# Attention and mixture of experts on one core: routing and expert slots in one block, half of the kept row added into each slot output

## The reference

```python
x = _layernorm(x + attention(x, ...))                 # x: (4, 512, 512)
top_vals, top_idx = jax.lax.top_k(x_flat @ w_router, 2)
probs = softmax(top_vals)                             # two gates per token
h = square(relu(einsum('nc,ecd->ned', x_flat, w_fc)))
y = einsum('ned,edc->nec', h, w_proj)
x = _layernorm(x + sum over the two experts of probs * y)
```

## Time and profile before

| what | value |
|---|---|
| median of 3 runs | 1528.96 us (1528.15 to 1529.29) |
| profiled execution, its own time | 1526.92 us |
| span of the profile | 1525.3 us |
| PE, PEld busy | 94%, 79% |
| DVE, ACT, POOL busy | 50%, 48%, 28% |
| mean granted clock of PE | 0.974 |
| accumulating gathers, issue to landing | 5.4 / 5.9 / 6.2 us |
| output stores of 256 KB, median issue to landing | 2.2 us |
| 2 MB weight loads, raw and rounded, median issue to landing | 9.4 and 8.3 us |

### The profile page before, as it was taken

How to read it: one execution, slowest core, us unless ns; L and a number is a source line. 1 busy time by engine, 2 the same in 40 slices (tenths; PEclk the granted TensorE clock), 3 DMA queues, 4 the chain that set the end, 5 groups by cost and what they waited for, 6 DMA issues and landing times. The chain is left out here.

```text
span 1525.3 us, 26299 instructions
## 1 busy us (share of the span) xinstructions
PE 1429.1 (94%) x7936; PEld 1210.1 (79%) x7937; DVE 770.0 (50%) x1784; ACT 728.3 (48%) x1633; POOL 421.5 (28%) x417
## 2 busy tenths in 40 slices
PE   7999999999999999999999998799999579999980
PEld 5888888888888888888888887588888468888870
DVE  6555555655555655655655554345545433333323
ACT  5655565655655655655655655222222123333333
POOL 1221212211222121221221211143233333543376
PEclk9999999999999999999999999899999789999995
DMA  4112112021111121111111120735445267556499
GB/s 154 50 40 62 36 53 62 28 62 48 41 62 48 41 62 48 41 48 62 41 48 62 41 70 21 274 143 206 170 173 190 93 214 248 193 190 237 150 180 207
DMA packets 71979, 160.23 MB, mean 105 GB/s; under 512 B 14096, under 2 KB 14736, under 8 KB 69520
## 3 DMA queue, kind: packets, MB, share of 16 engines
q1 hardware_dynamic: 61168, 109.55, 22.0%
q0 software_dynamic: 10784, 50.36, 11.0%
HBM read 107.36 MB, written 52.52 MB: 105 GB/s over the span
## 5 line engine op out<-in xcount | busy, mean ns | idle before, releaser
L317 POOL TENSOR_TENSOR small<-small,half 128x4 f32<-128x4 f32 x193 | 194.6, 1008 | 761.8 <-DVE small L346 761.8
L434 DVE CUSTOM_DVE_ANT_0 logit<-score_ps,bias 128x128 f32<-128x128 f32 (+3 forms) x256 | 124.8, 487 | 156.8 <-PE score_ps L531 118.8
L269 ACT ACTIVATE prob<-logit,small 128x128 f32<-128x128 f32 (+3 forms) x256 | 144.2, 563 | 118.5 <-DVE small L434 114.7
L544 PEld LDWEIGHTS y_ps<-vs,prob_t 128*128 128x128 f32 x1280 | 174.9, 191 | 21.9 <-ACT prob_t L276 4.5
L544 PE MATMUL y_ps<-vs,prob_t 128*128 (+1 forms) x1280 | 185.2, 276 | 1.0 <-ACT prob_t L276 0.7
L276 ACT ACTIVATE prob_t<-prob_ps 128x128 f32<-128x128 f32 (+3 forms) x256 | 111.5, 436 | 53.3 <-PE prob_ps L537 52.3
L766 ACT ACTIVATE yt_hi<-turn_ps,subln 128x512 fp32r<-128x512 f32 x64 | 44.0, 688 | 168.8 <-PE turn_ps L1031 156.2
L537 PE MATMUL prob_ps<-ident,prob 128*128 128x128 f32 x640 | 112.8, 274 | 3.3 <-ACT prob L269 3.2
L488 PE MATMUL k_ps<-w_hi,x_hi 128*128 (+1 forms) x256 | 103.9, 406 | 5.9 <-DVE w_lo L385 5.8
L1040 PE MATMUL out_ps<-w_hi,yt_hi 128*128 128x512 f32 x256 | 107.5, 420 | 1.9 <-DVE yt_lo L872 1.9
L488 PE MATMUL v_ps<-w_hi,x_hi 128*128 (+1 forms) x256 | 107.0, 418 | 0.0
(11 more groups left out here) (174 smaller groups left out, 3268.3 us busy)
## 6 DMA issues: line engine op xcount, KB each, us to landing
y_scratch<-x_now SPq DMA_DIRECT2D x65, 256.0 KB, 2.9
x_raw<-in_x_t SPq DMA_DIRECT2D x64, 256.0 KB, 2.8
y_raw<-y_scratch SPq DMA_DIRECT2D x15, 1024.0 KB
w_raw<-in_w_experts POOLq DMA_DIRECT2D x7, 2048.0 KB, 9.4
w_hi<-in_w_experts POOLq DMA_DIRECT2D x7, 2048.0 KB, 8.3
w_raw<-in_w_all SPq DMA_DIRECT2D x16, 768.0 KB, 5.6
slots_y<-zeros SPq DMA_DIRECT2D x13, 768.0 KB
xs<-slots_x SPq DMA_DIRECT2D x39, 256.0 KB
```

The source lines that it names most:

```text
L269: nc.scalar.activation(prob[:, 0:width], logit[:, 0:width], ACT.Exp, scale=-1.0, bias=least[:, h:h + 1], accum_out=row_sum[:, (i % 2) * HG ...
L317: nc.gpsimd.tensor_tensor(r, ms, half[:, :], ALU.pow).then_inc(ready, 1)
L434: nc.vector.tensor_tensor_reduce(out=logit[:, 0:width], in0=score_ps[:, 0:width], in1=bias[:, h, T - width:T], scale=1.0, scalar=3e38, op0 ...
L544: mm = nc.tensor.matmul(y_ps[:, h * D:(h + 1) * D], prob_t[:, j * P:(j + 1) * P], one(vs[:, bass.ds(now, 1), j, h * D:(h + 1) * D]), start ...
```

## The change

Five things change together.

1. The second and third block become one, `mixture_phase`: the functions of each engine for routing and for slots run one after the other without a barrier between. PSUM and SBUF tensors of the routing are used again by the slots.
2. `layernorm` yields half the row (variance times 4 before the power of -1/2), so the rows scattered to the slots are x1/2. The router's gap is doubled in the exponential and the gates are multiplied by 4. The output of a slot becomes gate times expert output plus the slot's input row, in one DVE operation; the sum of a token's two slots then holds x1 itself. ACT's copy to `x1` (`keep_x1`) and its evacuation (L1320) are gone.
3. The first gathers are plain copies without accumulation, and gather t waits until gather t - 2 has landed. The second ones still add; gather t waits for t - 8.
4. `xs` has four buffers. A row load waits for the slot's output instead of PE's turn, and is issued behind the store; before the first experts' loads POOL waits for four row loads instead of two.
5. In the last norm POOL's power works on groups of 4, 4, 4, 2 and 2 tiles, the first two placed behind the issue of gathers 8 and 12; DVE scales the mean in the same groups. The last scatter of rows is issued ahead of the gates of the last two tiles.

```diff
-            def keep_x1(t, b):
+            def keep_x1_t(t):
                 act.wait_ge(x1_turned, t + 1)
                 nc.scalar.activation(x1_t[:, :], x1_ps[:, :], ACT.Copy).then_inc(x1_t_ready, 1)
-                out = x1[:, t, :] if isinstance(t, int) else one(x1[:, bass.ds(t, 1), :])
-                nc.scalar.activation(out, x1_now[:, b, :], ACT.Copy).then_inc(x1_kept, 1)
 
             def second_weight(t, b):
...
-                nc.scalar.activation(second[:, b:b + 1], src, ACT.Exp).then_inc(second_ready, 1)
+                nc.scalar.activation(second[:, b:b + 1], src, ACT.Exp, scale=2.0).then_inc(second_ready, 1)
...
             def inverse_std(t):
                 pool.wait_ge(var_ready, t + 1)
-                nc.gpsimd.tensor_tensor(var_eps[:, :], mean_var[:, 1:2], eps[:, :], ALU.add).then_inc(var_biased, 1)
+                pool.nop(nofuse=True)
+                nc.gpsimd.tensor_scalar(var_eps[:, :], mean_var[:, 1:2], EPS, 4.0, ALU.add, ALU.mult).then_inc(var_biased, 1)
                 pool.wait_ge(var_biased, t + 1)
                 nc.gpsimd.tensor_tensor(rstd[:, :], var_eps[:, :], half[:, :], ALU.pow).then_inc(rstd_ready, 1)
...
             inverse_std(NT - 1)
             dispatch(NT - 2, 0)
+            dispatch(NT - 1, 1)
             send_gates(NT - 2, 0)
-            dispatch(NT - 1, 1)
             send_gates(NT - 1, 1)
 
-        @block.vector
...
-                    dve.wait_ge(x1_kept, t - 1)
+                    dve.wait_ge(x1_turned, t - 1)
                     dve.wait_ge(dispatched[b], sent)
                 nc.vector.tensor_scalar(x1_now[:, b, :], res[:, :], mean_var[:, 0:1], rstd[:, 0:1],
                                         ALU.subtract, ALU.mult).then_inc(x1_ready, 1)
@@ -916,7 +908,7 @@
             def gates(t, b):
 
                 dve.wait_ge(second_ready, t + 1)
-                nc.vector.tensor_scalar(either[:, :], second[:, b:b + 1], 1.0, None, ALU.add).then_inc(either_ready, 1)
+                nc.vector.tensor_scalar(either[:, :], second[:, b:b + 1], 1.0, 0.25, ALU.add, ALU.mult).then_inc(either_ready, 1)
                 dve.wait_ge(either_ready, t + 1)
                 nc.vector.reciprocal(gate_now[:, b, 0:1], either[:, :]).then_inc(first_share, 1)
...
+        xs, yo = y_raw[:, 0, :, :], y_raw[:, 1, :, :]
         hid = sb("hid", [P, 2, F])
-        ht_hi = sb("ht_hi", [P, 2, F], F32R)
-        ht_lo = sb("ht_lo", [P, 2, F], F32R)
...
-        step = sem("slot_step")
+        xt_ps, h_ps = turn_ps[0:2], turn_ps[2:4]
+        ht_ps, ye_ps = [out_ps[0], x1_ps], [out_ps[1], router_ps]
...
-            def load_rows(at, b):
-                sp.dma_start(xs[:, b, :], rows_of(x_slots[bass.ds(at, 1), :, :])).then_inc(xs_loaded[b], 16)
+            def load_rows(at, y):
+                sp.dma_start(xs[:, y, :], rows_of(x_slots[bass.ds(at, 1), :, :])).then_inc(xs_loaded[y], 16)
 
             def load_gates(at, y):
                 sp.dma_start(gs[:, y:y + 1], rows_of(g_slots[bass.ds(at, 1), :, :])).then_inc(g_loaded[y], 16)
@@ -1196,10 +1162,7 @@
                     sp.wait_ge(padded[k], 16)
                 else:
                     sp.wait_ge(padded[EARLY_PADS], 16 * (E - EARLY_PADS + 1))
-                at = tile_at(k)
-                if k >= 2:
-                    sp.wait_ge(xs_turned, k - 1)
-                load_rows(at, k % 2)
+                load_rows(tile_at(k), k)
                 if k == 1:
                     for e in range(EARLY_PADS, E):
                         pad(sp, e)
@@ -1211,15 +1174,12 @@
             def slot_step(k, b, h, y, q):
                 if more(k, 4):
                     at = tile_at(k + 4)
-                if more(k, 4):
-                    sp.wait_ge(xs_turned, k + 3)
-                    sp.nop(nofuse=True)
-                    load_rows(at, b)
                 sp.wait_ge(yo_ready, k + 1)
                 sp.nop(nofuse=True)
-                out = y_slots[k] if isinstance(k, int) else rows_of(y_slots[bass.ds(k, 1), :, :])
+                out = y_slot[k] if isinstance(k, int) else rows_of(y_slot[bass.ds(k, 1), :, :])
                 sp.dma_start(out, yo[:, y, :]).then_inc(yo_stored[y], 16)
                 if more(k, 4):
+                    load_rows(at, y)
                     load_gates(at, y)
 
             sp.wait_ge(y_cleared, 16 * CLEAR_STEPS)
...
-            for b in range(2):
-                pool.wait_ge(xs_loaded[b], 16)
+            for y in range(YB):
+                pool.wait_ge(xs_loaded[y], 16)
             for e in (1, 2):
                 load_and_split(e, None)
             pool.wait_ge(tables_known, 1)
@@ -1270,28 +1229,33 @@
             pool.wait_ge(slots_known, 1)
             stored_up_to(E - 2)
             for t in range(NT):
+                if t >= 2:
+                    pool.wait_ge(first_gathered[t % 2], 16 * (t // 2))
                 pool.indirect_dma_start(x1[:, t, :], None, slots_y,
-                                        bass.IndirectOffsetOnAxis(ap=slot_y[:, 0, t:t + 1], axis=0),
-                                        compute_op=ALU.add).then_inc(first_gathered, 16)
+                                        bass.IndirectOffsetOnAxis(ap=slot_y[:, 0, t:t + 1], axis=0))\
+                    .then_inc(first_gathered[t % 2], 16)
             stored_up_to(E - 1)
-            pool.wait_ge(first_gathered, 16 * NT)
+            def end_inverse_std(first, last):
+                pool.wait_ge(end_var_biased, last)
+                nc.gpsimd.tensor_tensor(end_rstd[:, first:last], end_var[:, first:last], end_half[:, 0:last - first],
+                                        ALU.pow).then_inc(end_rstd_ready, last - first)
+
+            pool.wait_ge(end_set_up, 1)
+            for b in range(2):
+                pool.wait_ge(first_gathered[b], 16 * (NT // 2))
             for t in range(NT):
+                if t >= GB:
+                    pool.wait_ge(second_gathered[t % GB], 16 * (t // GB))
                 pool.indirect_dma_start(x1[:, t, :], None, slots_y,
                                         bass.IndirectOffsetOnAxis(ap=slot_y[:, 1, t:t + 1], axis=0),
-                                        compute_op=ALU.add).then_inc(second_gathered[t], 16)
-
-            pool.wait_ge(set_up, 1)
-            for t in range(NT):
-                if t % 2 == 1 and t < NT - 2 or t >= NT - 2:
-
-                    n = 2 if t < NT - 2 else 1
-                    part = slice(t + 1 - n, t + 1)
-                    pool.wait_ge(var_biased, t + 1)
-                    nc.gpsimd.tensor_tensor(rstd[:, part], var_eps[:, part], half[:, 0:n], ALU.pow)\
-                        .then_inc(rstd_ready, n)
-
-        @block.scalar
-        def _(act):
+                                        compute_op=ALU.add).then_inc(second_gathered[t % GB], 16)
+                if t in BETWEEN:
+                    end_inverse_std(t - 2 * RB, t - RB)
+            end_inverse_std(NT - 2 * RB, NT - RB)
+            end_inverse_std(NT - RB, NT - 2)
+            end_inverse_std(NT - 2, NT)
...
-                act.wait_ge(down_done, k + 1)
-                act.wait_ge(yo_stored[y], q * 16 + 16)
-                act.wait_ge(g_loaded[y], q * 16 + 16)
-                nc.scalar.activation(yo[:, y, :], ye_ps[b][:, :], ACT.Copy, scale=gs[:, y:y + 1]).then_inc(yo_ready, 1)
...
+                dve.wait_ge(yo_stored[y], q * 16 + 16)
+                dve.wait_ge(g_loaded[y], q * 16 + 16)
+                nc.vector.scalar_tensor_tensor(yo[:, y, :], ye_ps[b][:, :], gs[:, y:y + 1], xs[:, y, :],
+                                               ALU.mult, ALU.add).then_inc(yo_ready, 1)
...
-            def scale_mean(t):
-                dve.wait_ge(rstd_ready, t + 1)
-                nc.vector.scalar_tensor_tensor(minus_mean[:, t:t + 1], mean_var[:, t, 0:1], -1.0, rstd[:, t:t + 1],
-                                               ALU.mult, ALU.mult).then_inc(mean_ready, 1)
+                dve.wait_ge(end_var_ready, t + 1)
+                nc.vector.tensor_scalar(end_var[:, t:t + 1], end_mean_var[:, t, 1:2], EPS, None, ALU.add)\
+                    .then_inc(end_var_biased, 1)
+
+            def scale_mean(first, last):
+                dve.wait_ge(end_rstd_ready, last)
+                nc.vector.scalar_tensor_tensor(minus_mean[:, first:last], end_mean_var[:, first:last, 0], -1.0,
+                                               end_rstd[:, first:last], ALU.mult, ALU.mult)\
+                    .then_inc(mean_ready, last - first)
 
             for t in range(NT):
-                dve.wait_ge(second_gathered[t], 16)
-                nc.vector.bn_stats(stats[:, t % 2, :], x1[:, t, :]).then_inc(stats_done, 1)
+                dve.wait_ge(second_gathered[t % GB], 16 * (t // GB + 1))
+                nc.vector.bn_stats(end_stats[:, t % 2, :], x1[:, t, :]).then_inc(end_stats_done, 1)
                 if t >= 1:
                     bias_variance(t - 1)
-                if t >= 3:
-                    scale_mean(t - 3)
```

(49 more changed lines are left out.)

127 lines of the change are left out of this document (54 added, 73 removed).

## The result

The changed kernel takes **1531.41 us** (median of 12 runs, 1529.59 to 1533.28), the kernel before 1527.95 in 12 runs beside it: a ratio of **1.0024**, 95% interval 1.0015 to 1.0032. It is slower, by 0.24% or 3.5 us at the medians: little, but clear of the noise. The forecast was 1525.3, faster by 3.7.

The account below looks back on a forecast made before the run. PE was taken as full, with the weight chain just under it and gathers and norm setting the end. Of 8 us won there, 2.2 pay for weights; span end 1521.6 against 1525.3, so 1528.96 less 3.7: 1525.3 us, range 1522.5 to 1528.5.

Parts of the forecast that it names:

- signs of failure: Whole prediction: fails if the weight chain moves over 2 us, PE never waits for weights, or gather issue-to-landing exceeds 3.5.
- Gathers, L = 3.0: First gathers: L, issue to landing of a plain gather, is 3.0 us (bounds 2.7 and 5.96); phase 27.3 against 34.4.
- The sum of the pairs: First gathers, two under way: each pair takes L + 0.25, so 7 x 3.25 + 1.3 + 3.0 + 0.25 = 27.3 us.
- Rival B: First gathers: flight 2.6 instead of 2.0, L = 3.6, phase 32.1, time 1529.5, nothing measurable; chance 0.20.
- rival C: First gathers: flight 4.4 like accumulating ones, L = 5.4, phase 46.5, time 1543.9; decides from L = 3.9; chance 0.20.
- Late row loads, priced "0, at most 2": Slots: row loads issued only 8.1 us before PE's turn, not 12; hidden in the wait before tile 22; 0, at most 2.
- PE waits for expert 5's weights, +2.2: Tile 22: PE arrives near 1364.4, waits until 1370.4, then slow clock costs 2.5; delay +2.2 us, range -2.3 to +4.5.
- First row load, 2.5 us to land: Gap before the first slot: load issued at 1215.9, 6.3 us earlier, about 2.5 to land; gap near 10, not 16.
- The issue of a plain gather: First gathers: a plain gather of 128 rows is issued in 1.0 us, against 1.54 for an accumulating one.
- the lump on ACT: Last norm: ACT's last eight rows come in a lump after tile 15, taking 6.4 us.
- the length of the second phase: End: second gathers start at 1474.1, issued every 1.85 us, and with the norm the span ends at 1521.6.
- the estimate of 5 us from the shared SBUF ports: Slots: by the skill alone, some ten new DVE overlaps could cost expert 5's weight chain 0.5 us each, 5 in all.

Follow-up runs that it names:

- six_early: weights_early with row buffers shared out as six for input rows and two for outputs, so row loads go two slots earlier: 1528.67 us, 0.9999 of the kernel before.
- weights_early: Changed kernel with POOL waiting for two row loads, not four, ahead of its weight loads: 1532.16 us, 1.0024 of the kernel before.
- no_row_wait: Changed kernel with zeros added in place of the slot's input row and each row load issued one slot earlier: 1532.50 us, 1.0023 of the kernel before.
- shift_128: Changed kernel with 128 unused bytes ahead of y_raw: 1529.33 us, 1.0003 of the kernel before.
- gates_late: Changed kernel with POOL's last four gate scatters held until the first two row loads landed: 1535.39 us, 1.0043 of the kernel before.
- best_end_gates: Changed kernel with weights after two row loads, no gather limit, 128-byte shift, reordered end, last gate scatters behind first w_hi load: 1522.20 us, 0.9955 of before.
- before_placed: Kernel before with 384 unused bytes ahead of xt_hi, placing operands as in the changed kernel modulo 512: 1530.67 us, 1.0015 of the kernel before.
- free_first: Changed kernel without first gather t's wait for gather t - 2: 1528.00 us, 0.9993 of the kernel before.

## Why the prediction was wrong, by its own steps

**How far off, and where.** The time of 1531.41 lies above the forecast's own range of 1522.5 to 1528.5. The forecast put the end of the span at 1521.6; it came at 1531.6. Of these 10 us, 3.4 lie ahead of the first gather (1450.24, not 1446.8), 7.9 in the first gathers (35.2, not 27.3), and the rest went 1.4 better (46.15, not 47.5). Two priced steps failed most, the landing of a gather and the late row loads, and one term was missing, the place of the operands. All three signs of failure that the prediction names came true: expert 5's subtraction ended 3.5 us later (1373.09 beside 1369.58), PE never waited for weights, and L was 3.9 in the mean, over 3.5.

**Gathers, L = 3.0.** This term was mis-sized, and it is the largest part. L was 3.3 to 3.9 and once 5.64, and a pair took 4.2, not 3.25. The sum of the pairs was right: put in 4.2 - 0.25 = 3.95 and it gives 34.9 for the 35.2 measured. The phase was to win 7 us and won nothing. Rival B (3.6, phase 32.1) was too low as well, and the mean lies at the 3.9 from which rival C was to decide; C's flight of 4.4 was reached once (5.64 - 0.95 = 4.7). Why a plain gather lands later than a plain store is not shown. The sum by the Trainium skill, DMA: Bandwidth & Descriptors, Anatomy of one DMA, was an estimate of 2.6 us of flight for 256 KB; the first gather's 3.44 - 1.01 = 2.4 agrees, the later ones with 2.4 to 3.0 still roughly, and 4.7 does not.

**Late row loads, priced "0, at most 2".** They cost 4.0 us in the profiled execution and 3.8 in six_early against weights_early, and without them (and with the weight chain started early) the kernel is as fast as the one before (0.9999). So it is without the limit on gathers alone (0.9993). Mending either of the two brings the change level with the kernel before, and no further; leaving the late row loads out without the early weight chain does not (no_row_wait, 1.0023). The prediction had both numbers side by side, 8.1 us between a row load's issue and its turn, and landings up to 9.9 beside a weight transfer. It let them hide in a wait for weights at tile 22; they came at slots 6 and 15, ahead of it, and at 24. A 2 MB load is under way for some 18 of every 30 us, so that the load of every few slots falls into the start of one.

**PE waits for expert 5's weights, +2.2.** It did not, since PE was late itself. The weight chain began later than forecast (1233.64, not 1228.5: the fourth row load waits for all pads, and the third and fourth are issued over 5.81 us), yet ended 0.56 before PE arrived (subtraction over at 1373.09, tile 22 at 1373.65). The mechanism was right and masked: as soon as row loads or the pitch are mended, the wait appears (no_row_wait, shift_128), with the slow clock behind it, 1.8 us in no_row_wait for the 2.5 that was charged.

**First row load, 2.5 us to land.** The issue was 1217.02, 1.1 after the forecast by the 1.1 that routing ended later. The landing took 6.63, of which some 4 are the scatters of gates: the gap is 10.2 and 9.9 in the two runs without them ahead of the load (gates_late, best_end_gates) and 13.2 to 15.4 in all others of the changed kernel. The gap became 14.0 us, not about 10. The prediction followed SP's queue alone and priced nothing for the scatters that POOL had issued just before.

**Not thought of: the place of the operands.** `ht_hi` and `xt_hi` share memory with `yt_hi` now and stand elsewhere. 0.065 us a step is 2.0 us by tile 31, and before_placed measured 2.3 for it over the whole kernel.

**Right.** The issue of a plain gather (0.95 to 1.01), the lump on ACT (5.76 for eight), the length of the second phase within 1.4 us (46.15 for 47.5), DVE's operation (0.75) at no cost by itself. The weight chain's subtractions did not stretch (1.29 median, 1.78 worst, as in the earlier trace rows), so the estimate of 5 us from the shared SBUF ports was not borne out.

The sum by measured parts: gap -2.2, row loads +3.8, place +2.3, gathers and end +0.7: +4.6, against +3.5 at the medians. It mixes ratios with one trace, and leaves out the 1.1 us by which routing ended later and the 0.7 in slots 12, 21 and 30. What stays open: why an operand's place changes the matmul's pitch, and why these four scatters keep a load of another queue from moving; both are shown only by their effect.

## What to carry to other kernels

When a buffer gets a second reader later in the step, work out how long before its use the next load can be issued, and set it against the landing beside the largest transfer in flight, not against the median. Count packets there and not bytes: where two queues take turns, 128 short rows last as long as 128 long ones. Then give it another buffer, as the six rows did. Where two chains lie at one height (here PE and the weights), a repair of either measures nothing: lift both before you judge one. Before a pair of transfers is limited to two under way, divide landing by issue: 3.4 and 1.26 ask for three, and the median of 4.8 that free_first showed with no limit for four (estimates; neither limit was run). And compare the pitch of untouched instructions whenever tensors move.

## What the runs showed of the hardware

- A 256 KB load of SP issued 0.3 to 1.0 us behind a 2 MB load of POOL landed 8.5 to 8.75 us after its issue, with the 2 MB, where its median is 3.4. The Trainium skill, DMA: Bandwidth & Descriptors, Queues, rings and completion order, has each engine take turns between queues packet by packet. This trace agrees, with 112 packets of each queue in the same 5 us, but the packets were of 16 KB and 2 KB, so the turns were equal and the bytes were not.
- Four scatters of 128 elements of 4 bytes, issued just ahead, held the next load for about 4 us: its first 16 packets are recorded with 3.1 us each (in gates_late its first 28 with 0.14), and for 2 us nothing moved.
- The same twelve fp32r matmuls took 2.80 or 2.77 us by a shift of their operands, of 128 bytes in the changed kernel and of 384 in the one before.
- A plain indirect gather of 256 KB is issued in 0.95 and lands 3.3 to 3.9 us after with two under way (once 5.64), and 3.3 to 6.0 with no limit; an accumulating one takes 1.54 and 5.96.
